# Second layer's experts: gate and bias on an expert's finished sum, second product as three rounded products, first products three blocks ahead

## The chip, the cores and the metric

One core of a Trainium2 chip runs the whole program. The time is that of one execution on the device, in microseconds (us). The engines named are TensorE (PE; its weight loads are shown apart as PEld), VectorE (DVE), ScalarE (ACT), GpSimd (POOL) and SyncE (SP), which issues the transfers.

## The reference

Four samples of 1024 tokens with 128 features go through two layers, each an attention and a mixture of experts, with a layer norm behind each of the four. The change touches the second layer's experts alone:

```
rh = gelu(x @ rW1 + rb1); p = softmax(rh @ rW2 + rb2)        # router, exact gelu
expert_weights, expert_indices = top_k(p, 2)                  # 2 of E = 4 experts
combine_w = (one_hot * expert_weights[..., None]).sum(axis=2)
for e in range(E):
    xi = x * token_mask[..., e:e + 1]
    h = gelu(xi @ We1[e] + be1[e])                            # 128 -> 512, exact gelu
    yo = h @ We2[e] + be2[e]                                  # 512 -> 128
    out = out + yo * combine_w[..., e:e + 1]                  # 0 for experts not chosen
x = layernorm(x + out)
```

All inputs and the result are float32.

## The kernel before

**Tiles and stages.** The kernel runs: first attention, the first layer's end (its output projection, norm, experts), second attention, the second layer's end. An end works on 8 chunks of 512 tokens, features on the partitions. Its experts are computed densely: 4 experts of 512 hidden features are 16 blocks of 128, n = 0 to 15, four to an expert. A block is three things: `pe_hidden` (L951) on TensorE, three rounded (float32r) matmuls that add up upper and lower halves of weights and inputs (w_hi x_hi, w_lo x_hi, w_hi x_lo) into one of four PSUM banks `hbank`; the Gelu `act_s` with bias be1 on ScalarE (L1134); and `hid`, act_s times the gate row of the expert, on VectorE (L1317). The second product (L1060) then adds w x hid in plain float32 to bank 0, over all 16 blocks, behind a bias matmul (L1058, be2 times the gates). ScalarE copies the finished sum to `y_sb` (L1141).

**Gate rows.** The router's gates of a token stand on its partition. `pe_gate_rows` (L964) spreads the gates of expert e, turned to rows in `gate_t`, over all partitions with a matmul against `expert_row` into bank 1 (L969), and ScalarE copies it to `gate_bc` (L1124). It is done at step 4e - 2, for expert 0 at step 15 of the chunk ahead.

**Order of the work.** Each engine runs its instructions in the order in which the code issues them, with semaphores between engines. `pe_chunk` (L1040), `act_chunk` (L1126) and `dve_chunk` (L1299) go through steps n = 0 to 15. At a step TensorE does its side work (`pe_beside`), a gate row, the first product of block n + h_lead (2), and the second product of block n. Side work of two other chunks is spread over the steps by `plan[1]`: for the chunk behind (back) y_turn (L979, transposes of y_sb to tokens; VectorE then adds the residual and takes statistics, L1235, L1162, L1165) and norm2 (L1170, into x_out, which SP stores); for the chunk ahead (front) os_ (L1270, a copy of the attention's output, one step before o_turn), o_turn (L890), o_proj (L1008, then on VectorE two additions and statistics, L1275, L1278), norm (L1170 into xs), x_turn (L890; ScalarE writes xt and x_hi, L1101, L1102, VectorE x_lo, L1286), hidden (L1018, the router's first product, with two Gelus rh, L1106), router (L1031, 16 small matmuls; VectorE subtracts the maximum), the exponentials e_sm on ScalarE one step later (L1113, an own table), weigh and spread on VectorE (L1207 to L1224), g_turn (L1037, then gate_t, L1116). GpSimd works out rstd from the statistics (L1348, L1349).

The stage begins in `pe_end` and its likes with the front half of chunk 0, during which ScalarE makes the upper half of the first weight, `w_hi` (L1150), and VectorE the lower, `w_lo` (L1332); SP has issued the loads of the weights we1 and we2 at L1419 and L1420. It ends with the back half of chunk 7.

Of the kernel before, what the change touches and what calls it, by code (L numbers as in the profile page):

```python
# [7 lines left out]
ALU = mybir.AluOpType  # L8
# [6 lines left out]
P = 128  # L15
# [25 lines left out]
SB = 3  # L41
PAIR_HEADS = (2, 0, 3, 1)
# [161 lines left out]
def build_program(nc, d, out):  # L204
    with ExitStack() as ctx:
# [35 lines left out]
        be2 = sb("be2", [2 * E0, D])  # L241
# [38 lines left out]
        with ExitStack() as overlay:  # L280
# [9 lines left out]
            act_s = [osb(f"act_s{i}", [P, CH]) for i in range(2)]  # L290
            lin_u = [osb(f"lin_u{i}", [P, CH]) for i in range(2)]
# [16 lines left out]
            with ExitStack() as layer_only:  # L308

                rh = layer_only.enter_context(nc.sbuf_tensor("rh", [P, 2, CH], F32))  # L310
                we2 = layer_only.enter_context(nc.sbuf_tensor("we2", [P, NH, P], F32))
# [11 lines left out]
        we2_loaded = sem("we2_loaded")  # L323
# [14 lines left out]
        class Stage:  # L338


            def __init__(self, n):
# [590 lines left out]
        for pl, steps in ((plan[0], (1, 3, 4, 5, 6, 7, 8, 9, 10, 11, None, 12, 13, 14)),  # L932
                          (plan[1], (1, 2, None, None, None, None, 2, 4, 6, 8, 10, 11, 12, 14))):
# [6 lines left out]
        h_banks, h_lead = [2, 4], [1, 2]  # L940
# [10 lines left out]
        def pe_hidden(pe, st, c, par, n, layer):  # L951

            pe.wait_ge(st.s_done, c * SPC + n + 1)
# [4 lines left out]
            for k in range(2 if layer == 0 else 1):  # L958
                for a, (w, x) in enumerate(((w_hi[k], x_hi[par]), (w_lo[k], x_hi[par]), (w_hi[k], x_lo[par]))):
                    last = nc.tensor.matmul(hbank[2 * k + n % h_banks[layer]], w[:, slice_of(n)], x[:, :], start=(a == 0),  # L960
# [11 lines left out]
        def pe_beside(pe, st, n, back, front, par, layer):  # L972

            pl = plan[layer]
            if back is not None:
                if n == pl.y_turn:
                    pe.wait_ge(st.y_saved, back + 2)
                    for t in range(TPC):
# [20 lines left out]
            if front is not None:  # L999
                if n == pl.o_turn:  # L1000
                    pe.wait_ge(st.o_in, front + 1)
                    pe_turn_tiles(bank[3], os_).then_inc(st.o_turned, 1)
# [36 lines left out]
                if n == SPC - 1:  # L1039
                    pe_gate_rows(pe, st, front, 0, layer)  # L1040

        def pe_chunk(pe, st, c, par, back, front, layer):
            per = SPC // n_exp[layer]
            w = w3 if layer == 0 else we2
            for n in range(SPC):
                pe_beside(pe, st, n, back, front, 1 - par, layer)
                e = n // per + 1
                if n % per == per - 2 and e < n_exp[layer]:
                    pe_gate_rows(pe, st, c, e, layer)
# [5 lines left out]
                if n == 0:  # L1055
                    pe.wait_ge(st.y_saved, c + 1)
                    if layer == 1:
                        nc.tensor.matmul(bank[0][:, :], be2[:, :], gate_t[:, :].bitcast(F32), start=True, stop=False)  # L1058
                pe.wait_ge(st.hid_ready, c * SPC + n + 1)
                nc.tensor.matmul(bank[0][:, :], w[:, n, :], hid[n % 2][:, :], start=(layer == 0 and n == 0),  # L1060
                                 stop=(n == SPC - 1)).then_inc(st.y_done, 1)

        def pe_end(pe, st, layer):
# [18 lines left out]
        def act_beside(act, st, n, back, front, par, layer):  # L1082
# [12 lines left out]
            if front is not None:  # L1095
# [203 lines left out]

        def dve_chunk(dve, st, c, par, back, front, layer):  # L1300
            per = SPC // n_exp[layer]
            for n in range(SPC):
                e = n // per
                if n % per == 0:
                    dve.wait_ge(st.gbc_saved, 1 + c * n_exp[layer] + e + 1)
                wait_used(dve, st.y_done, c * SPC + n - 1)
                if layer == 0:
                    dve.wait_ge(st.h_ready, c * SPC + n + 1)
# [6 lines left out]
                else:  # L1315
                    dve.wait_ge(st.s_done, h_banks[layer] + c * SPC + n + 1)
                    nc.vector.tensor_tensor(hid[n % 2][:, :], act_s[n % 2][:, :], gate_bc[e % 2][:, :],  # L1317
                                            ALU.mult).then_inc(st.hid_ready, 1)
                dve_beside(dve, st, n, back, front, 1 - par, layer)

        def dve_end(dve, st, layer):
# [18 lines left out]
            dve_chunk(dve, st, 2 * B - 1, 1, 2 * B - 2, None, layer)  # L1340
            for n in range(SPC):
# [32 lines left out]
        def _(sp):  # L1374
# [45 lines left out]
            sp.dma_start(we2[:, :, :], d["we2"]).then_inc(we2_loaded, 16)  # L1420
# [103 lines left out]
def _layout(i):  # L1524
# [38 lines left out]
    o["be2"] = np.zeros((2 * E0, D), f)  # L1563
    o["be2"][0:E1] = o["be2"][E0:E0 + E1] = a["L1_ffn_be2"]
# [14 lines left out]
```

## Time and profile before

| what | us |
|---|---|
| median of 3 runs | 1924.15 (1923.0 to 1927.66) |
| profiled execution | 1922.64 |
| its span | 1920.8 |
| TensorE busy | 1743.9 |
| VectorE busy | 1389.2 |
| ScalarE busy | 1162.8 |
| stage of the change, from os_ of chunk 0 | 1568.2 to the end |

The time of an execution is its span and 1.8 us around it. A busy share is an average over stages: what an edit is worth is read in its own stage, from what each engine waits for there. Matmuls are pipelined; the distance from one start to the next says more than the length of one. An f32 matmul of the program is shown as two instructions, a rounded one as one. The row of L513 is another stage's and stands for its kind of operation.

### The profile page before, as it was taken

The page shows a single profiled execution, that of the slowest core. Times are in us where ns is not written, and L with a number is a line of the kernel's source. Part 1 is how long each engine was busy: PE and PEld are TensorE (multiplying, and loading weights), DVE is VectorE, ACT ScalarE, POOL GpSimd, SP SyncE. Part 2 cuts the span into 40 slices and gives each one's busy share as a digit, 9 for nine tenths or more (in the row PEclk, how much of TensorE's full clock was granted, in tenths as well). Part 3 has the DMA queues.
Part 4 walks back from the last instruction along what each step waited for, and adds up shares of the span by engine and source line. Part 5 has one row for each costly group of instructions (what it writes and reads, how often), then busy time and mean ns, then how long its engine had stood idle before and what let it go on. Part 6 is the DMA issues. An engine that isn't in the chain of part 4 may idle for free.

```text
span 1920.8 us, 31169 instructions
## 1 busy us (share of the span) xinstructions
PE 1743.9 (91%) x9328; PEld 844.8 (44%) x9328; DVE 1389.2 (72%) x2540; ACT 1162.8 (61%) x1801; POOL 97.0 (5%) x123
## 2 busy tenths in 40 slices
PE   6899999699999999579999999999999968988997
PEld 3334343366656656333333333333333325544553
DVE  3788888757777777478889888989898814455544
ACT  3888888544344444107777777777777754444443
POOL 1000000001111011010000000000000000011000
PEclk9899999889999999859999999999999988999999
DMA  7532121101111000210000000000100010000000
GB/s 220 140 92 60 49 62 47 66 1 34 33 33 33 29 10 28 66 41 22 22 23 21 22 21 21 22 22 21 37 26 21 2 44 1 6 6 11 5 5 11
DMA packets 44844, 68.99 MB, mean 36 GB/s; under 512 B 15952, under 2 KB 25056, under 8 KB 44144
## 3 DMA queue, kind: packets, MB, share of 16 engines
q1 hardware_dynamic: 44784, 68.28, 11.9%
q8 instruction: 26, 0.43, 0.1%
q14 instruction: 34, 0.28, 0.1%
HBM read 42.04 MB, written 26.21 MB: 36 GB/s over the span
## 4 chain that ended last, share of the span: by engine, by line
PE 70%; DVE 12%; ACT 9%; issue 5%; SPq 1%; DMA 1%; POOL 1%; DVEq 1%; ACTq 0%; POOLq 0%
PE full_o L689 13%; PE score L676 12%; PE hid_pair L960 11%; PE bank L1060 9%; ACT probs L738 6%; PE causal_o L451 5%; PE triple L435 4%; PE max_pair L652 3%; DVE cprobs L514 2%; PE bank L969 2%; PE bank L990 2%; DVE hid L1317 1%; PE bank L890 1%; PE max_pair L663 1%; DVE negmax L776 1%
## 5 line engine op out<-in xcount | busy, mean ns | idle before, releaser
L776 DVE TENSOR_REDUCE negmax<-max_pair 128x1 f32<-128x1024 f32 x512 | 599.9, 1218 | 69.4 <-PE max_pair L652 62.3
L738 ACT ACTIVATE probs<-score 128x512 f32<-128x512 f32 x1024 | 529.0, 603 | 150.8 <-PE score L676 150.8
L652 PE MATMUL max_pair<-k_st,q_st 64*128 64x512 f32 x1024 | 405.3, 474 | 22.2 <-DMA q_st<-q_scr 18.1
L676 PE MATMUL score<-q_st,k_st 64*128 64x512 f32 x1024 | 382.9, 451 | 34.0 <-ACT probs L738 24.6
L676 PEld LDWEIGHTS score<-q_st,k_st 64*128 64x128 f32 x1024 | 170.6, 185 | 304.7 <-ACT probs L738 284.9
L484 ACT ACTIVATE cprobs<-triple 128x1536 f32<-128x1536 f32 x192 | 268.5, 1456 | 38.5 <-PE triple L435 38.3
L689 PE MATMUL full_o<-probs,v_st 128*32 128x512 f32 x2048 | 272.9, 606 | 0.0
L960 PE MATMUL hid_pair<-x_hi,w_hi 128*128 128x512 f32 x384 | 206.8, 539 | 0.0
L652 PEld LDWEIGHTS max_pair<-k_st,q_st 64*128 64x128 f32 x1024 | 171.7, 191 | 79.5 <-DVE negmax L776 39.5
L1132 ACT ACTIVATE act_s<-hid_pair 128x512 f32<-128x512 f32 x128 | 76.4, 597 | 157.5 <-PE hid_pair L960 157.4
L514 DVE TENSOR_SCALAR cprobs<-cprobs 128x1536 f32<-128x1536 f32 (+6 forms) x272 | 163.0, 624 | 0.4 <-ACT cprobs L484 0.4
L451 PE MATMUL causal_o<-cprobs,v_st 128*32 128x512 f32 (+3 forms) x1536 | 154.5, 498 | 8.4 <-DVE o_sb L539 7.0
L1060 PE MATMUL bank<-hid,we 128*128 128x512 f32 x256 | 137.0, 618 | 20.4 <-DVE hid L1317 20.4
L960 PE MATMUL hid_pair<-x_lo,w_hi 128*128 128x512 f32 x384 | 154.0, 401 | 0.0
L960 PE MATMUL hid_pair<-x_hi,w_lo 128*128 128x512 f32 x384 | 153.6, 400 | 0.0
L435 PE MATMUL triple<-q_st,k_st 64*128 64x512 f32 (+3 forms) x768 | 143.8, 400 | 8.3 <-ACT cprobs L484 5.0
L1317 DVE TENSOR_TENSOR hid<-act_s,gate_bc 128x512 f32<-128x512 f32 x128 | 85.1, 688 | 90.8 <-ACT act_s L1134 79.2
L1309 DVE TENSOR_TENSOR lin_u<-hid_pair,gate_bc 128x512 f32<-128x512 f32 x128 | 88.3, 690 | 74.9 <-PE hid_pair L960 68.9
L1060 PE MATMUL bank<-hid,w 128*128 128x512 f32 x256 | 132.2, 598 | 0.9 <-DVE hid L1313 0.7
L435 PEld LDWEIGHTS triple<-q_st,k_st 64*128 64x128 f32 x768 | 73.5, 187 | 116.0 <-issue 64.8
L513 DVE SCALAR_TENSOR_TENSOR cprobs<-cprobs,bound 128x512 f32<-128x512 f32 (+4 forms) x176 | 94.9, 539 | 16.0 <-ACT cprobs L484 10.5
L1124 ACT ACTIVATE gate_bc<-bank 128x512 f32<-128x512 f32 x96 | 57.4, 598 | 79.7 <-PE bank L969 79.5
(129 smaller groups left out, 1594.0 us busy)
## 6 DMA issues: line engine op xcount, KB each, us to landing
k_st<-k_scr SPq DMA_DIRECT2D x64, 128.0 KB, 2.8
q_st<-q_scr SPq DMA_DIRECT2D x128, 64.0 KB, 2.3
q_st<-q_scr SPq DMA_DIRECT2D x16, 512.0 KB
k_st<-k_scr SPq DMA_DIRECT2D x64, 104.0 KB
q_scr<-qk_hi SPq DMA_DIRECT2D x24, 256.0 KB, 2.9
k_scr<-qk_hi SPq DMA_DIRECT2D x24, 256.0 KB, 3.1
q_scr<-qk_lo SPq DMA_DIRECT2D x16, 256.0 KB, 2.9
k_scr<-qk_lo SPq DMA_DIRECT2D x16, 256.0 KB, 3.2
```

Of the source, the lines that this page charges most:

```text
L435: last = nc.tensor.matmul(triple[n % 2][:, bk, off:off + w], k_st[p][rows, j, kt * P:(kt + 1) * P], q_st[p][rows, q0:q0 + w], start=True, ...
L451: last = nc.tensor.matmul(causal_o[SLOT * j:SLOT * (j + 1), c0:c0 + w], v_st[p][:, kt, j, :], cprobs[at % CP][:, bk, off:off + w], start=( ...
L484: nc.scalar.activation(cprobs[n % CP][:, :, :], triple[n % 2][:, :, :], ACT.Exp, scale=SCALE).then_inc(L.exp_done, 1)
L514: ins = nc.vector.tensor_scalar(plain, plain, float(np.exp(-CLIP)), float(np.exp(CLIP)), ALU.max, ALU.min)
L652: ins = nc.tensor.matmul(ring[slot][:, half, :], q_st[p][rows, qt * P:(qt + 1) * P], k_st[p][rows, j, half * CH:(half + 1) * CH], start=Tr ...
L676: nc.tensor.matmul(sbank[L.score_bank(e)][:, :], k_st[p][rows, j, kt * P:(kt + 1) * P], q_st[p][rows, q0:q0 + w], start=True, stop=True, t ...
L689: last = nc.tensor.matmul(full_o[SLOT * j:SLOT * (j + 1), :], v_st[p][:, kt, j, :], probs[s % NP][:, j, :], start=(kt == 0), stop=last_ste ...
L738: nc.scalar.activation(probs[s % NP][:, j, :], sbank[L.score_bank(e)][:, :], ACT.Exp, scale=SCALE).then_inc(L.exp_done, 1)
L776: nc.vector.tensor_reduce(negmax[:, qt // TPC, j, qt % TPC:qt % TPC + 1], ring[slot][:, :, :].rearrange("p a n -> p (a n)"), AXX, ALU.max, ...
L960: last = nc.tensor.matmul(hbank[2 * k + n % h_banks[layer]], w[:, slice_of(n)], x[:, :], start=(a == 0), stop=(a == 2))
L1060: nc.tensor.matmul(bank[0][:, :], w[:, n, :], hid[n % 2][:, :], start=(layer == 0 and n == 0), stop=(n == SPC - 1)).then_inc(st.y_done, 1)
L1317: nc.vector.tensor_tensor(hid[n % 2][:, :], act_s[n % 2][:, :], gate_bc[e % 2][:, :], ALU.mult).then_inc(st.hid_ready, 1)
```

## The change

The second weight we2 is now split into upper and lower halves like we1, and so is hid: on even blocks ScalarE writes the rounded upper half `hid_hi` itself with a second Gelu from the same bank, on odd blocks VectorE copies it from act_s; VectorE then writes `hid_lo` = act_s - hid_hi. There are four buffers of each. The gate is not applied to hid any more: an expert's four blocks are summed alone, into bank 0 for even experts and hbank[3] for odd ones, and `dve_weigh` adds the bias be2 (a column now, transposed on the host side of the layout) and multiplies by the gate row; experts 1 to 3 go through `y_tmp` and an addition into y_sb. The weighing of expert e stands at step 4e + 5, that of expert 3 at step 1 of the next chunk. First products run three blocks ahead in three banks (`h_of`, `h_apart`: where two blocks that use one bank are two apart, the wait is for the Gelu two before). Gate row e is made at step 4e + 2. y_turn moves from step 1 to 3, norm2 from 2 to 5, g_turn from 14 to 15. The bias matmul and ScalarE's copy of y_sb go in this layer.

```diff
-                          (plan[1], (1, 2, None, None, None, None, 2, 4, 6, 8, 10, 11, 12, 14))):
+                          (plan[1], (3, 5, None, None, None, None, 2, 4, 6, 8, 10, 11, 12, 15))):
...
-        h_banks, h_lead = [2, 4], [1, 2]
+        h_banks, h_lead = [2, 3], [1, 3]
+
+        y_bank = [bank[0][:, :], hbank[3]]
+        h_of = [[n % 2 for n in range(SPC)], [n % 3 if n < SPC - 1 else 1 for n in range(SPC)]]
+        h_apart = [[2] * SPC, [2 if n in (1, SPC - 1) else 3 for n in range(SPC)]]
...
-            pe.wait_ge(st.s_done, c * SPC + n + 1)
+            pe.wait_ge(st.s_done, c * SPC + n + 1 + h_banks[layer] - h_apart[layer][n])
...
                     pe.wait_ge(st.y_saved, back + 2)
+                    if layer == 1 and front is not None:
+                        pe.wait_ge(st.ot_ready, front + 1)
...
                     pe.wait_ge(st.o_in, front + 1)
+                    if layer == 1 and back is not None:
+                        pe.wait_ge(st.gate_t, front)
...
+        def pe_gate_step(pe, st, c, n, layer):
+            per = SPC // n_exp[layer]
+            e = n // per + (layer == 0)
+            if n % per == per - 2 and e < n_exp[layer]:
+                pe_gate_rows(pe, st, c, e, layer)
...
+        def pe_split_product(pe, st, c, n):
+            per = SPC // E1
+            e, f = n // per, n % per
+            if f == 0:
+                wait_used(pe, st.y_used, c * E1 + e - 1)
+            pe.wait_ge(st.hid_ready, c * SPC + n + 1)
+            hi, lo = hid_hi[n % HB], hid_lo[n % HB]
+            for a, (w, x) in enumerate(((w_hi[1], hi), (w_lo[1], hi), (w_hi[1], lo))):
+                last = nc.tensor.matmul(y_bank[e % 2], w[:, slice_of(n)], x[:, :], start=(f == 0 and a == 0),
+                                        stop=(f == per - 1 and a == 2))
+            last.then_inc(st.y_done, 1)
...
-                    if layer == 1:
-                        nc.tensor.matmul(bank[0][:, :], be2[:, :], gate_t[:, :].bitcast(F32), start=True, stop=False)
...
             act.wait_ge(st.gbc_ready, c * n_exp[layer] + e + 1)
-            wait_used(act, st.hid_ready, c * SPC + (e - 1) * (SPC // n_exp[layer]))
+            if layer == 0:
+                wait_used(act, st.hid_ready, c * SPC + (e - 1) * (SPC // E0))
+            else:
+                wait_used(act, st.y_used, c * E1 + e - 1)
...
-                    nc.scalar.activation(act_s[n % 2][:, :], hbank[n % h_banks[1]], ACT.Gelu,
+                    if n % 2 == 0:
+                        wait_used(act, st.y_done, c * SPC + n - HB + 1)
+                        nc.scalar.activation(hid_hi[n % HB][:, :], hbank[h_of[1][n]], ACT.Gelu, bias=be1[:, n:n + 1])
+                    nc.scalar.activation(act_s[n % 2][:, :], hbank[h_of[1][n]], ACT.Gelu,
                                          bias=be1[:, n:n + 1]).then_inc(st.s_done, 1)
...
-                    for k in range(2 if layer == 0 else 1):
-                        act.wait_ge(raw_loaded[k], 16 * (layer + 1) if k == 0 else 16)
+                    for k in range(2):
+                        act.wait_ge(raw_loaded[k], 16 * (layer + 1))
...
+        def dve_weigh(dve, st, c, e):
+            dve.wait_ge(st.gbc_saved, 1 + c * E1 + e + 1)
+            dve.wait_ge(st.y_done, c * SPC + (e + 1) * (SPC // E1))
+            if e == 0:
+                wait_used(dve, st.y_turned, c)
+            elif e > 1:
+                dve.wait_ge(st.y_sum, 2 * c + e - 1)
+            nc.vector.scalar_tensor_tensor((y_sb if e == 0 else y_tmp)[:, :], y_bank[e % 2], be2[:, e:e + 1],
+                                           gate_bc[e % 2][:, :], ALU.add, ALU.mult).then_inc(st.y_used, 1)
+            if e > 0:
+                dve.wait_ge(st.y_used, c * E1 + e + 1)
+                nc.vector.tensor_tensor(y_sb[:, :], y_sb[:, :], y_tmp[:, :],
+                                        ALU.add).then_inc(st.y_sum if e < E1 - 1 else st.y_saved, 1)
...
+                    wait_used(dve, st.y_done, c * SPC + n - HB + 1)
                     dve.wait_ge(st.s_done, h_banks[layer] + c * SPC + n + 1)
-                    nc.vector.tensor_tensor(hid[n % 2][:, :], act_s[n % 2][:, :], gate_bc[e % 2][:, :],
-                                            ALU.mult).then_inc(st.hid_ready, 1)
+                    if n % 2 == 1:
+                        nc.vector.tensor_copy(hid_hi[n % HB][:, :], act_s[n % 2][:, :]).then_inc(st.odd_hi, 1)
+                        dve.wait_ge(st.odd_hi, c * (SPC // 2) + n // 2 + 1)
+                    nc.vector.tensor_tensor(hid_lo[n % HB][:, :], act_s[n % 2][:, :], hid_hi[n % HB][:, :].bitcast(F32),
+                                            ALU.subtract).then_inc(st.hid_ready, 1)
+                    if n % per == 1 and (n > per or back is not None):
+                        dve_weigh(dve, st, c if n > per else back, (e - 1) % E1)
...
-                    for k in range(2 if layer == 0 else 1):
+                    for k in range(2):
                         dve.wait_ge(w_upper, 2 * layer + k + 1)
...
-            sp.dma_start(we2[:, :, :], d["we2"]).then_inc(we2_loaded, 16)
+            sp.dma_start(w_raw[1][:, :], d["we2"].rearrange("p n c -> p (n c)")).then_inc(raw_loaded[1], 16)
```

## Rows read from the trace of the kernel before

**Rows 1.** The page, busy time of each engine and the granted clock.

```profile
PE 1743.9 (91%) x9328; PEld 844.8 (44%) x9328; DVE 1389.2 (72%) x2540; ACT 1162.8 (61%) x1801; POOL 97.0 (5%) x123
...
PEclk9899999889999999859999999999999988999999
```

**Rows 2.** Windows cut at the router's product: busy, (instructions), clock, DMA share, GB/s.

```profile
1625.20:1666.56 41.36, 37.93 (x134) 21.09 (x132) 21.25 (x70) 18.89 (x31) 3.65 (x4) 0.96 0.02 7
1666.56:1706.90 40.34, 36.27 (x133) 20.23 (x132) 21.37 (x70) 18.77 (x31) 3.63 (x4) 1.00 0.03 8
```

**Rows 3.** Waits, 1621 to 1866 us: total us, times, longest.

```profile
PEld bank L1060 <- DVE hid L1317: 32.0, 30, 2.2
...
PEld bank L890 <- DVE os_ L1270: 10.8, 6, 1.8
```

**Rows 4.** Groups of instructions by form, 1621 to 1866 us; the last one of the whole span.

```profile
L1317 DVE TENSOR_TENSOR hid<-act_s,gate_bc 128x512 f32<-128x512 f32 x96 | 63.8, 687 | 61.0 <-ACT act_s L1134 56.1 <-PE bank L1060 4.0
L1134 ACT ACTIVATE act_s<-hid_pair,be 128x512 f32<-128x512 f32 x96 | 62.3, 689 | 19.3 <-PE hid_pair L960 12.6 <-DVE hid L1317 6.6
...
L1058 PE MATMUL bank<-gate_t,be 16*128 16x512 f32 x12 | 6.7, 640 | 0.0
...
L513 DVE SCALAR_TENSOR_TENSOR cprobs<-cprobs,bound 128x512 f32<-128x512 f32 x48 | 32.8, 684 | 0.0
```

**Rows 5.** Timeline: two blocks in a row (start us, length us, engine).

```profile
1605.25 1.02 PE L1060 MATMUL bank<-hid,we 128*128 128x512 f32 x2
...
1606.35 0.40 PE L960 MATMUL hid_pair<-x_hi,w_lo 128*128 128x512 f32 x1
...
1606.58 0.40 PE L960 MATMUL hid_pair<-x_lo,w_hi 128*128 128x512 f32 x1
...
1606.82 1.02 PE L1060 MATMUL bank<-hid,we 128*128 128x512 f32 x2
```

**Rows 6.** Timeline: TensorE's side work: o_proj, a gate row and what follows, the router's two products.

```profile
1607.68 1.05 PE L1008 MATMUL bank<-w_o,ot 128*128 128x128 f32 x8
...
1613.41 0.49 PE L969 MATMUL bank<-gate_t,expert_row 16*128 16x512 f32 x1
...
1614.17 0.39 PE L960 MATMUL hid_pair<-x_hi,w_lo 128*128 128x512 f32 x1
...
1621.15 1.88 PE L1018 MATMUL bank<-xt,rw 128*128 128x512 f32 x4
...
1625.04 1.84 PE L1031 MATMUL bank<-rw,rh 128*128 128x4 f32 x16
```

**Rows 7.** Timeline: ScalarE at the exponentials, beside the router.

```profile
1626.00 1.28 ACT L1113 ACT_TABLE_LOAD   x1
...
1627.54 0.22 ACT L1113 ACTIVATE e_sm<-sc 128x16 f32<-128x16 f32 x1 [0.26 <-DVE sc L1186]
...
1629.07 1.27 ACT L1134 ACTIVATE act_s<-hid_pair,be 128x512 f32<-128x512 f32 x2
```

**Rows 8.** Timeline: VectorE's side work in steps 1, 4 and 6.

```profile
1640.17 0.69 DVE L1235 TENSOR_TENSOR res<-xs,bank 128x512 f32<-128x512 f32 x1 [1.05 <-PE bank L979]
...
1642.21 0.39 DVE L1270 COPY os_<-o_tm 128x512 f32 x1
...
1648.62 0.69 DVE L1275 TENSOR_TENSOR res<-x_tm,bank 128x512 f32<-128x512 f32 x1 [1.70 <-PE bank L1008]
...
1651.38 1.28 DVE L1317 TENSOR_TENSOR hid<-act_s,gate_bc 128x512 f32<-128x512 f32 x2
...
1653.60 1.11 DVE L1170 TENSOR_SCALAR xs<-res,mv,rstd 128x128 f32<-128x128 f32 x4 [0.93 <-POOL rstd L1349]
```

**Rows 9.** The second weight's load (KB, us to landing), w_lo at the start, and y_sb at the end.

```profile
we<-in_we SPq DMA_DIRECT2D x1, 1024.0 KB, 7.4
...
1578.28 2.28 DVE L1332 TENSOR_TENSOR w_lo<-w_raw,w_hi 128x2048 fp32r<-128x2048 f32 x1
...
1911.17 0.60 ACT L1141 ACTIVATE y_sb<-bank 128x512 f32<-128x512 f32 x1 [2.08 <-PE bank L1060]
```

More of the change, by code:

```diff
@@ L290, in build_program @@
             act_s = [osb(f"act_s{i}", [P, CH]) for i in range(2)]
+            with ExitStack() as layer_only:
+                hid_hi = [layer_only.enter_context(nc.sbuf_tensor(f"hid_hi{i}", [P, CH], F32R)) for i in range(HB)]
             lin_u = [osb(f"lin_u{i}", [P, CH]) for i in range(2)]
@@ L310, in build_program @@
                 rh = layer_only.enter_context(nc.sbuf_tensor("rh", [P, 2, CH], F32))
-                we2 = layer_only.enter_context(nc.sbuf_tensor("we2", [P, NH, P], F32))
+                hid_lo = [layer_only.enter_context(nc.sbuf_tensor(f"hid_lo{i}", [P, CH], F32R)) for i in range(HB)]
+                y_tmp = layer_only.enter_context(nc.sbuf_tensor("y_tmp", [P, CH], F32))
         q_scr0 = nc.dram_tensor("q_scr0", [B, P, 2, T], F32, kind="Internal").ap()
@@ L959, in pe_hidden @@
                 for a, (w, x) in enumerate(((w_hi[k], x_hi[par]), (w_lo[k], x_hi[par]), (w_hi[k], x_lo[par]))):
-                    last = nc.tensor.matmul(hbank[2 * k + n % h_banks[layer]], w[:, slice_of(n)], x[:, :], start=(a == 0),
+                    last = nc.tensor.matmul(hbank[2 * k + h_of[layer][n]], w[:, slice_of(n)], x[:, :], start=(a == 0),
                                             stop=(a == 2))
@@ L1054, in pe_chunk @@
                     pe_hidden(pe, st, front, 1 - par, lead - SPC, layer)
-                if n == 0:
-                    pe.wait_ge(st.y_saved, c + 1)
-                    if layer == 1:
-                        nc.tensor.matmul(bank[0][:, :], be2[:, :], gate_t[:, :].bitcast(F32), start=True, stop=False)
-                pe.wait_ge(st.hid_ready, c * SPC + n + 1)
-                nc.tensor.matmul(bank[0][:, :], w[:, n, :], hid[n % 2][:, :], start=(layer == 0 and n == 0),
-                                 stop=(n == SPC - 1)).then_inc(st.y_done, 1)
+                if layer == 0:
+                    if n == 0:
+                        pe.wait_ge(st.y_saved, c + 1)
+                    pe_product(pe, st, c, n)
+                else:
+                    pe_split_product(pe, st, c, n)
         def pe_end(pe, st, layer):
@@ L1066, in pe_end @@
                 pe_beside(pe, st, n, None, 0, 0, layer)
-            pe.wait_ge(w_lower, 2 if layer == 0 else 3)
-            if layer == 1:
-                pe.wait_ge(we2_loaded, 16)
+            pe.wait_ge(w_lower, 2 * (layer + 1))
             for n in range(h_lead[layer]):
@@ L1116, in act_beside @@
                     nc.scalar.activation(gate_t[:, :], bank[3][0:2 * E0, :], ACT.Copy).then_inc(st.gate_t, 1)
-                if n == SPC - 1:
+                if n == SPC - 1 and layer == 0:
                     act_gate_rows(act, st, front, 0, layer)
@@ L1303, in dve_chunk @@
                 e = n // per
[L1304 to L1306 removed]
                 if layer == 0:
+                    if n % per == 0:
+                        dve.wait_ge(st.gbc_saved, 1 + c * n_exp[layer] + e + 1)
+                    wait_used(dve, st.y_done, c * SPC + n - 1)
                     dve.wait_ge(st.h_ready, c * SPC + n + 1)
@@ L1340, in dve_end @@
             dve_chunk(dve, st, 2 * B - 1, 1, 2 * B - 2, None, layer)
+            if layer == 1:
+                dve_weigh(dve, st, 2 * B - 1, E1 - 1)
             for n in range(SPC):
```

31 lines of the change are left out of this document (18 added, 13 removed).

## The prediction

> **What bounds the kernel now.** I read the page first [rows 1]: TensorE is busy for 91% of the span, VectorE for 72%, ScalarE for 61%. These shares mix four stages; the edits touch the second layer's expert stage alone, the last 325 us. So I cut that stage at the first router product (L1031) of each chunk [rows 2]. The first cut to the last is 1625.20 to 1870.22, six chunks, 40.84 us each. Two lengths alternate: 41.5 us where the granted clock is 0.96 and 40.2 us where it is 1.00, so one stretch at the lower level (1.2 of 2.4 GHz) costs some 1.3 us. VectorE works 21.3 us of such a chunk, ScalarE 18.8; TensorE is the busy one.
>
> The waits of these six chunks [rows 3] say what TensorE's idle time is: the second product L1060 waits for hid 30 times, 32.0 us, and the first transposes of the o tiles for VectorE's copy, 10.8 us. The timeline [rows 5] gives the bare block: L1060 starts at 1605.25, the next at 1606.82, so 1.57 us. A rounded matmul takes 0.23 us (1606.35 to 1606.58), a triple 0.69, so L1060 in f32 takes 1.57 - 0.69 = 0.88 us. Sixteen blocks are 25.1 us; the work beside them, read in the same way [rows 6], is 0.9 for the o projection, 1.7 for the router's first product, 1.8 for its second, 0.6 for each of four gate rows (from 1613.35, where the product before ends, to 1613.94, where the next triple starts: its second matmul stands at 1614.17), and 0.45 for each of four groups of four transposes, half of the o projection's eight matmuls: 8.6 us. With the bias matmul (0.9) that is 34.6; the other 5.6 of a 40.2 us chunk are waits.
>
> **What the change takes from TensorE.** The second product becomes three rounded matmuls, 0.69 for 0.88: 16 x 0.19 = 3.0 us a chunk. The bias matmul L1058 (two instructions a chunk, [rows 4]) goes: 0.9. TensorE's own work falls from 34.6 to 30.7 us. If nothing else bound, eight chunks would give 31 us.
>
> **What it puts on VectorE.** The hid product becomes the subtraction hid_lo: same shape, 0.69 long, 0.61 from start to start (two in 1.29). Added for each of 8 odd blocks is a rounding copy and a wait for it. The trace has no 128x512 rounding copy on VectorE. Its bounds are the f32 copy from SBUF, 0.39 to 0.42 [rows 8], and the one-element-a-cycle operation, 0.69; I take 0.42 plus 0.04, as the operands lie in SBUF. The Trainium skill ("VectorE: DVE Perf Modes", What auto-detection actually checks) makes the faster mode a matter of one source, both sides in SBUF, not of the type's name; by it the copy is 0.42, by the slow bound each chunk has 8 x 0.27 = 2.2 us more on VectorE. Four weighings a chunk are a scalar_tensor_tensor (0.68, [rows 4]) and an addition 0.61 to 0.69, with the wait 1.35 together: 5.4 us. So VectorE goes from 21.3 to about 21.3 + 3.7 + 5.4 = 30.4 us, as much as TensorE's 30.7. ScalarE gets 8 Gelus more (0.58 each) and loses one copy: 18.8 to 23. Two engines of 30.5 us that feed each other through buffers of 3 or 4 blocks don't run in 30.5; what counts is where they meet.
>
> **The walk through a chunk.** Time 0 is the end of the router's second product: 1.8 after 1625.04, so 1626.83 in the trace. Every latency is from the timeline: ScalarE starts 0.2 after a triple ends, 0.05 after a semaphore; gate_bc to the next act_s 0.48; a TensorE instruction that really waited loses 0.15 more, its weights not being loaded ahead.
>
> Steps 12 to 15. ScalarE has two Gelus for block 12 now and is done at 0 instead of -0.8. Loading Exp's table takes 1.28, e_sm 0.22, the Gelu table 1.28 [rows 7]: act_s 13 starts at 2.7 (before: 2.24) and ends at 3.4. Hidden block 15 shares its bank with block 13, so TensorE, free at 1.4, waits for that until 3.5. Product 12 ends at 5.0, 13 at 6.4, gate row 3 at 7.0. act_s 15 stands behind the gate_bc copy on ScalarE: 8.15; hidden 1 of the next chunk needs it and ends at 9.05, product 14 at 9.75. g_turn, 15 now, has its gates since 7.4; ends at 10.2, product 15 at 11.6. On ScalarE the two Gelus of block 0 stand behind the gate_t copy (10.25): done at 12.0; hidden 3 waits 0.6 for that. Product 1 ends at 15.0 (before it began at 13.84, so ended at 14.7). This far nothing is won.
>
> Steps 1 to 3. VectorE's hid_lo 1 is done at 13.7, weighing 3 at 15.1, the os_ copy behind it at 15.46; o_turn waits 0.5 (before: 1.1, behind the statistics). Gate_bc, act_s 3, copy and subtraction give hid 3 at 19.05, product 3 ends at 20.0.
>
> Steps 3 to 7 are VectorE's. From 19.0 it has no gap: y_turn's addition and statistics 2.04 (1640.17 to 1642.21), hid 4, the o projection's part 2.76 (1648.62 to 1651.38), hid 5 with its copy 1.08, weighing 0 1.35, norm2 1.05, hid 6, norm 1.05 (a 1.11 row, [rows 8]), hid 7 with its copy. So hid 4 is ready at 21.7, 5 at 25.5, 6 at 28.5, 7 at 30.6, and TensorE waits 0.3, 2.4, 1.0 and 0.7 us; product 7 ends at 31.5. The longer lead can't hide it: block n's Gelu is possible only once product n-3 is about to start, some 3 us ahead, and this stretch has 11.6 us on VectorE against 7.0 on TensorE (0.9 + 0.6 + four blocks of 1.38).
>
> Steps 8 to 10. x_turn ends at 31.95; xt and x_hi on ScalarE, then act_s 9 at 33.8, for which hidden 12 waits 0.6; hid 9 at 35.0; product 9 ends at 35.9, the router's first product at 37.6, and gate row 0.6, two triples' worth 1.38 and the second product 1.78 make 41.4. Against 40.84 that is **+0.56 a chunk**, six times: +3.4 us. (Against the chunks at full clock, 40.2, it is +1.2: 3.9 us won in work, 5.1 lost in waits.)
>
> **The ends of the stage.** Start: the first gate row falls out of the way to hidden 0, and product 0 ends about 1.5 us earlier; of this the step 5 and 9 waits of chunk 0, walked alike without y_turn and norm2, leave 0.6 at its router's end: -0.6. The second weight's DMA is the size of we2's and landed in 7.4 us, at 1575.8 [rows 9]; its w_hi copy of 1.9 us ends before x_turn's xt at 1579.57, and the second w_lo, 2.28 like the first, ends near 1583, under the router's products, long before hidden 0 at 1596.4: 0; uncovered it would be 2 us. Last chunk: no front half; walked alike product 15 ends 39.1 after its zero; before it was 39.3 (from 1871.85 to 1911.15, where y_sb follows, [rows 9]): -0.2. Then y_sb is not one copy (0.60 at 1911.17) but the last weighing, 1.35: +0.7.
>
> **The clock.** Low stretches come after TensorE's waits: the ones before follow product 5's wait. TensorE will wait about 10.7 us a chunk instead of 5.6, so I count one low stretch in every chunk; it falls partly where VectorE decides, so 0.5 of 1.3 us: +3.5 (bounds 0 and +9).
>
> **Sum.** 3.4 - 0.6 - 0.2 + 0.7 + 3.5 = +6.8 on the profiled execution's 1922.64 (span 1920.8 and 1.8 around it): 1929.4. It lies 1.5 below the median of 1924.15, so 1931 for the median, 0.35% slower. Differences under 0.3% (5.8 us) can't be told from none.
>
> **Rivals.** (A) The waits don't build up and TensorE's saving shows. It would be so if TensorE carried a lead into step 3: the waits of steps 4 to 7 (4.4 us) and for block 15 (2.1) halve, a chunk takes 38.2: seven times -2.6, 1905 to 1910. For it: half of the sum of before's waits is of the kinds that go (o tiles, y_sb before L1058). Against: ScalarE and VectorE work in a fixed order, and act_s 3 stands behind a gate_bc of step 2 whatever the lead. Chance 0.2. (B) It cancels: the Exp step costs less, as act_s 13 gets in sooner, a chunk takes 40.6 and the clock's term is near 0: 1921 to 1928. Chance 0.3. (C) the forecast, a chunk of 41 to 42 us: 1929 to 1937, chance 0.38. (D) As C but the rounding copy at 0.69: six of its eight (blocks 1, 3, 5, 7, 9, 13) are on the path, 6 x 0.27 = 1.6 a chunk, +11: 1942; chance 0.12. A ends on the other side; it decides from the point where hid 5 is ready less than 22.4 after the router.
>
> The likeliest is C, with its own range 1929 to 1937; 1905 to 1944 leaves out a part of A and of D. Slower 0.5, same 0.3, faster 0.2.
>
> **What would show it.** After the change: chunks, router to router, of 41 to 42 us; VectorE busy 30 us of each and without gaps from y_turn's addition to norm; second products 4 to 7 waiting for hid_lo, 4 to 5 us together; hidden block 15 waiting 2 us for act_s behind the Exp table. The copy's row reads 0.42 or 0.69 at once. Chunks under 40 us make it wrong, and so would a second product's triple that isn't 0.69 us.

## The result, and the profile after

The changed kernel takes 1942.36 us (median of 4 runs, 1937.9 to 1947.94) against 1923.58 us: a ratio of 1.0114, 95% interval 1.0093 to 1.0134, so slower by 1.1%. The forecast was 1931, slower by 0.35%. A second timing (e12 below) gave 1.0116.

The page of the changed kernel, as [rows 1] of before:

```profile
PE 1743.1 (90%) x9440; PEld 882.1 (45%) x9440; DVE 1454.3 (75%) x2661; ACT 1196.4 (61%) x1858; POOL 95.7 (5%) x123
...
PEclk8899999899999999759999999999999969889988
```

TensorE is as busy as before though it got less work. The profiled execution is the slowest of the four, 1947.94 us, 25.3 above the one of before. The same cut as [rows 2], at the first matmul of the router's second product (L1045 now, L1031 before). The first row is chunk 0 and the last row the last chunk with the tail (columns: us, then busy time and instructions of PE, PEld, DVE, ACT, POOL, granted clock, DMA share, GB/s):

```profile
1590.54:1629.72 39.18, 31.76 (x119) 23.23 (x119) 19.44 (x60) 18.19 (x30) 1.65 (x2) 0.79 0.00 1
1629.72:1672.99 43.27, 35.83 (x146) 24.91 (x145) 29.15 (x85) 22.80 (x38) 3.29 (x4) 0.92 0.02 7
1672.99:1717.57 44.58, 37.66 (x146) 25.89 (x144) 29.11 (x85) 22.83 (x38) 3.22 (x4) 0.89 0.02 6
1717.57:1762.55 44.98, 37.45 (x146) 25.85 (x145) 29.35 (x85) 22.95 (x38) 3.29 (x4) 0.89 0.02 7
1762.55:1804.08 41.53, 34.56 (x146) 23.86 (x145) 29.03 (x85) 22.82 (x38) 3.22 (x4) 0.96 0.02 7
1804.08:1847.43 43.35, 35.81 (x145) 24.61 (x144) 29.34 (x85) 22.93 (x38) 3.29 (x4) 0.92 0.02 7
1847.43:1891.96 44.53, 37.64 (x145) 25.82 (x144) 29.22 (x85) 22.80 (x38) 3.23 (x4) 0.89 0.02 6
1891.96:1946.10 54.14, 37.90 (x151) 25.79 (x149) 35.27 (x94) 25.01 (x40) 3.52 (x4) 0.87 0.03 10
```

The same two rows of the kernel before, chunk 0 and the last chunk with the tail:

```profile
1585.91:1625.04 39.13, 32.32 (x108) 19.59 (x109) 15.32 (x52) 15.59 (x25) 1.79 (x2) 0.83 0.00 1
...
1870.06:1920.80 50.74, 39.61 (x134) 21.57 (x132) 23.38 (x72) 19.86 (x31) 2.77 (x4) 0.96 0.04 11
```

The six whole chunks take 43.71 us on average (1629.72 to 1891.96) instead of 40.84: 6 x 2.87 = 17.2 us. The last chunk and tail take 54.1 instead of 50.7, 3.4. The stretch of chunk 0 is equal, 39.2 and 39.1. The other 4.6 us lie ahead of the stage of the change: its first instruction, the os_ copy of chunk 0, starts at 1572.87, before at 1568.24, and from there to the first row it is 17.67 us in both. The edits are to the second layer's experts, not to what runs ahead of them, and in the profiled executions of the experiments below it starts anywhere from 1563.7 (e8) to 1572.1 (e11), at 1570.3 in e12, the same kernel again. So these 4.6 us vary from one execution to another; what makes them vary isn't shown.

The column of the granted clock is what to read here. The chunks of 41.5, 43.3 and 44.5 to 45.0 us have a clock of 0.96, 0.92 and 0.89. A chunk at clock k has spent (1 - k) / 0.5 of its time at the lower level: 3.3, 6.9 and 9.8 us. Where these low stretches lie is seen in windows of 2 us. One in the first whole chunk, then one in the second:

```profile
1658.00:1660.00 2.00, 2.00 (x6) 1.09 (x5) 2.00 (x7) 0.63 (x2) 0.54 (x1) 0.61 0.00 0
...
1664.00:1666.00 2.00, 2.00 (x9) 1.61 (x9) 0.00 (x0) 0.45 (x1) 0.00 (x0) 0.68 0.00 0
...
1680.00:1682.00 2.00, 2.00 (x6) 1.59 (x5) 1.86 (x6) 0.00 (x0) 0.00 (x0) 0.50 0.00 0
```

Read through the whole stage, they lie at two places. One is behind product 5's wait, some 28 to 30 us into the chunk, in every chunk: 3.4 us long in the chunk from 1762.55 and 6.8 us in the five others (before, every second chunk had one of 3.4 there). The other is behind hidden 15's wait, some 5.5 us into the chunk: 3.4 us, in the second, third and sixth whole chunk and in the last. So the three kinds of chunk are product 5 short, product 5 long, and product 5 long with hidden 15. Why a stretch is long, and why the same wait of hidden 15 is followed by none in three chunks, isn't shown.

### The profile page after: what moved, and what is told of

It is laid out like the page before. It is cut to its first block and busy times, and to the rows that moved or that the text cites. A ratio compares the mean times of both kernels' runs of the same rounds, so it can differ in the third digit from the quotient of the medians.

```text
span 1946.1 us, 31707 instructions
## 1 busy us (share of the span) xinstructions
PE 1743.1 (90%) x9440; PEld 882.1 (45%) x9440; DVE 1454.3 (75%) x2661; ACT 1196.4 (61%) x1858; POOL 95.7 (5%) x123
## 5 line engine op out<-in xcount | busy, mean ns | idle before, releaser
L970 PE MATMUL hid_pair<-x_hi,w_hi 128*128 128x512 f32 x384 | 187.8, 489 | 28.2 <-ACT act_s L1173 28.2
L970 PEld LDWEIGHTS hid_pair<-x_hi,w_hi 128*128 128x128 f32 x384 | 75.5, 197 | 78.1 <-ACT act_s L1173 39.9
L1376 DVE TENSOR_TENSOR hid_lo<-act_s,hid_hi 128x512 fp32r<-128x512 f32 x128 | 88.0, 689 | 26.4 <-ACT act_s L1173 24.1
```

The lines of the kernel that those rows point to most:

```text
L970: last = nc.tensor.matmul(hbank[2 * k + h_of[layer][n]], w[:, slice_of(n)], x[:, :], start=(a == 0), stop=(a == 2))
```

## The walk against the trace

The chunk from 1762.55 is the one with the least time at the low level. TensorE's waits in it (timeline; the last bracket is the idle time before and its releaser), to be read from the router's end, 1762.55 + 1.78 = 1764.33:

```profile
1767.81 0.50 PE L970 MATMUL hid_pair<-x_hi,w_hi 128*128 128x512 f32 x1 [1.95 <-ACT act_s L1173]
...
1772.56 0.50 PE L970 MATMUL hid_pair<-x_hi,w_hi 128*128 128x512 f32 x1 [1.27 <-ACT act_s L1173]
...
1786.45 0.47 PE L1078 MATMUL hid_pair<-hid_hi,w_hi 128*128 128x512 f32 x1 [0.15 <-DVE hid_lo L1376]
...
1790.16 0.50 PE L1078 MATMUL hid_pair<-hid_hi,w_hi 128*128 128x512 f32 x1 [2.08 <-DVE hid_lo L1376]
...
1798.29 0.51 PE L970 MATMUL hid_pair<-x_hi,w_hi 128*128 128x512 f32 x1 [0.36 <-ACT act_s L1173]
...
1799.55 0.50 PE L1078 MATMUL bank<-hid_hi,w_hi 128*128 128x512 f32 x1 [0.30 <-DVE hid_lo L1376]
```

Hidden 15 starts at +3.48, hidden 1 at +8.23, product 4 at +22.1, product 5 at +25.8, hidden 12 at +34.0, product 9 at +35.2. The walk, with its 0.15 after a real wait, had 3.6, 8.35, 21.9, 25.7, 33.95 and 35.2. VectorE in steps 3 to 7, in the first whole chunk:

```profile
1650.69 0.68 DVE L1275 TENSOR_TENSOR res<-xs,bank 128x512 f32<-128x512 f32 x1
...
1653.08 0.69 DVE L1376 TENSOR_TENSOR hid_lo<-act_s,hid_hi 128x512 fp32r<-128x512 f32 x1
1653.69 0.68 DVE L1315 TENSOR_TENSOR res<-x_tm,bank 128x512 f32<-128x512 f32 x1
...
1656.45 0.41 DVE L1374 CAST hid_hi<-act_s 128x512 fp32r<-128x512 f32 x1
1656.89 0.69 DVE L1376 TENSOR_TENSOR hid_lo<-act_s,hid_hi 128x512 fp32r<-128x512 f32 x1
1657.50 0.74 DVE L1348 SCALAR_TENSOR_TENSOR y_sb<-bank,be,gate_bc 128x512 f32<-128x512 f32 x1
1658.16 1.11 DVE L1210 TENSOR_SCALAR x_out<-res,mv,rstd 128x128 f32<-128x128 f32 x4
1659.19 0.68 DVE L1376 TENSOR_TENSOR hid_lo<-act_s,hid_hi 128x512 fp32r<-128x512 f32 x1
1659.79 1.11 DVE L1210 TENSOR_SCALAR xs<-res,mv,rstd 128x128 f32<-128x128 f32 x4
1660.82 0.42 DVE L1374 CAST hid_hi<-act_s 128x512 fp32r<-128x512 f32 x1
```

From y_turn's addition to the copy of block 7, 10.1 us, VectorE is never idle for more than 0.21 us. The rounding copy is a CAST of 0.41 to 0.43 (the bound of 0.69 is out), the subtraction 0.69, and the weighing's first instruction 0.74, not the 0.68 of [rows 4], where all operands lie in SBUF.

## The experiments

Each ratio is against the kernel before on the same chip, with its 95% interval. "A chunk" is the mean of six, router to router, in the profiled execution.

**e1: unread matmuls in TensorE's waits.** The edit, with the wait on the last gate copy that keeps bank 1 free:

```diff
+        FILL = {5: 8, 6: 3, 7: 2, 12: 7}
+            pe.wait_ge(st.gbc_saved, c * E1 + (n - 3) // 4 + 2)
+            for _ in range(FILL[n]):
+                nc.tensor.matmul(bank[1][:, :], w_hi[0][:, slice_of(0)], x_hi[par][:, :], start=True, stop=True)
```

> The changed kernel with rounded 128x512 matmuls that nobody reads, put into bank 1 where TensorE waits: 8 before product 5's wait, 3 at the start of step 6, 2 before product 7's wait, 7 at the start of step 12 (0.23 us each at full clock, inside waits of 2 us that the changed kernel's trace shows). Theory K (what the forecast mis-sized is the clock: the low stretches behind these waits cost some 2 us a chunk): the granted clock in the stage rises from 0.90 to 0.96 or more, a chunk falls from 43.7 to about 42, the ratio to the kernel before from 1.0114 to 1.003 to 1.006. Rival W (the waits themselves are longer than the walk had them, the clock only follows): chunks stay at 43.5 or grow by what of the fillers sticks out, ratio 1.011 to 1.016.

1930.32 us, ratio 1.0059 (1.0044 to 1.0075). Its six chunks, and the last one:

```profile
1623.45:1664.79 41.34, 37.37 (x165) 26.38 (x164) 29.36 (x85) 22.80 (x38) 3.29 (x4) 1.00 0.02 7
1664.79:1705.94 41.15, 37.62 (x165) 26.39 (x164) 29.23 (x85) 22.80 (x38) 3.22 (x4) 1.00 0.02 7
1705.94:1747.44 41.50, 37.32 (x165) 26.38 (x164) 29.36 (x85) 22.96 (x38) 3.29 (x4) 1.00 0.03 8
1747.44:1788.54 41.10, 37.60 (x165) 26.38 (x164) 29.23 (x85) 22.79 (x38) 3.22 (x4) 1.00 0.02 7
1788.54:1830.02 41.48, 37.35 (x165) 26.38 (x164) 29.36 (x85) 22.95 (x38) 3.29 (x4) 1.00 0.02 7
1830.02:1871.11 41.09, 37.56 (x166) 26.39 (x165) 29.23 (x85) 22.80 (x38) 3.22 (x4) 1.00 0.02 7
1871.11:1927.30 56.19, 41.59 (x178) 29.60 (x176) 35.30 (x94) 25.01 (x40) 3.52 (x4) 0.92 0.03 10
```

TensorE does 20 matmuls more in each chunk, 4.6 us of them, and the chunk falls from 43.71 to 41.28, with the clock at 1.00 throughout. Nothing of the computation was taken away, and TensorE's 24 waits for the Gelu and 12 for hid_lo in the six chunks are still there, only shorter. So 2.4 us of each chunk were the clock's, and 41.3 is what the waits alone make of it: the walk had 41.4. In the last chunk the fillers stick out (56.2 against 54.1).

Chunk against the same chunk, this prices the low stretches of the changed kernel. The short one behind product 5 costs 0.4 us (41.53 against 41.10), the long one 1.9 (43.27 against 41.34, 43.35 against 41.48), and long with hidden 15's 3.4 to 3.5 (44.58, 44.98 and 44.53 against 41.15, 41.50 and 41.09). So the first 3.4 us behind product 5 cost 0.4, every further 3.4 us 1.5.

**e2: norm2 at step 10.** One number in the plan, 5 to 10.

> The changed kernel with one number changed: norm2 (1.05 us on VectorE, four tensor_scalars) from step 5 to step 10, where VectorE has slack. Theory D (steps 3 to 7 are VectorE's, as in the walk): blocks 6 and 7 are ready 1.05 us sooner, a chunk is 1.0 us shorter at the same clock, more if a low stretch goes too: ratio 1.0114 falls to about 1.007. Rival P (TensorE at its low clock sets the pace of these steps): no change, 1.010 to 1.012.

1938.34 us, 1.0102 (1.0088 to 1.0117): the time is the rival's (1.010 to 1.012), not the theory's 1.007, although the mean chunk fell to 42.65 (43.71 in the changed kernel, 43.18 in e12's execution of it). Two chunks of it, then two windows of 2 us in the second of them:

```profile
1668.11:1711.12 43.01, 36.07 (x146) 24.70 (x145) 29.23 (x85) 22.82 (x38) 3.16 (x4) 0.92 0.02 7
1711.12:1753.51 42.39, 34.71 (x146) 23.78 (x145) 29.36 (x85) 22.94 (x38) 3.24 (x4) 0.96 0.02 7
```

```profile
1717.00:1719.00 2.00, 2.00 (x6) 1.55 (x5) 1.93 (x4) 0.48 (x1) 0.00 (x0) 0.50 0.02 4
...
1741.00:1743.00 2.00, 2.00 (x8) 1.21 (x8) 1.99 (x6) 0.81 (x2) 0.59 (x1) 1.00 0.00 0
```

From product 5's start to the router's first product it takes 9.03 us, in the changed kernel's 1762.55 chunk 10.19: the 1.05 of norm2 are won where the walk said. But the chunk at 0.96 takes 42.4, not 41.5. Its low stretch lies at 1716 to 1720, just behind hidden 15's wait, where TensorE sets the pace: gate row 3 starts 8.0 after the router's end instead of 6.5. In the changed kernel's chunk at 0.96 it lies behind product 5's wait (1791 to 1795), where VectorE sets the pace by the walk, and costs the 0.4 of e1.

**e3: the second product in float32 again.** ScalarE writes the Gelu straight to four float32 buffers:

```diff
-            for a, (w, x) in enumerate(((w_hi[1], hi), (w_lo[1], hi), (w_hi[1], lo))):
+            nc.tensor.matmul(y_bank[e % 2], w_raw[1][:, slice_of(n)], hid_lo[n % HB][:, :], start=(f == 0),
...
-                    nc.vector.tensor_tensor(hid_lo[n % HB][:, :], act_s[n % 2][:, :], hid_hi[n % HB][:, :].bitcast(F32),
-                                            ALU.subtract).then_inc(st.hid_ready, 1)
```

> The changed kernel with its rounding undone: the second product is one float32 matmul of we2 with ScalarE's Gelu (four buffers, written straight by ScalarE), so VectorE has neither hid nor halves to make, ScalarE 16 Gelus instead of 24. Gate and bias on an expert's sum, the lead of three blocks and the plan stay. TensorE's own work is 33.7 us a chunk, VectorE's 21.3 - 9.8 + 5.4 = 17. Theory D (VectorE and ScalarE in series with TensorE set the chunk): the waits of steps 4 to 7 go, a chunk takes 36 to 38 us, and the kernel 1893 to 1907, ratio 0.984 to 0.991, better than both. Rival T (TensorE's work counts first): 3 us more work a chunk than the changed kernel, so slower than it, above 1.012.

1893.57 us, 0.987 (0.9856 to 0.9885), faster than both kernels. A chunk, and TensorE's two long waits in it:

```profile
1657.09:1693.92 36.83, 34.10 (x129) 20.28 (x128) 15.91 (x61) 17.95 (x30) 2.53 (x4) 1.00 0.03 8
```

```profile
1661.86 0.50 PE L970 MATMUL hid_pair<-x_hi,w_hi 128*128 128x512 f32 x1 [1.27 <-ACT hid_lo L1170]
...
1666.92 0.50 PE L970 MATMUL hid_pair<-x_hi,w_hi 128*128 128x512 f32 x1 [1.26 <-ACT hid_lo L1170]
```

The three rounded products save TensorE 3 us a chunk; leaving them out saves 43.71 - 36.84 = 6.9, of which 2.4 are the clock's (e1) and 4.4 are left with both at 1.00. VectorE has 16.0 us of work instead of 29.2, and the waits for hid are gone. What is left are the waits of hidden 15 and hidden 1 for ScalarE.

**e4: the lead of three alone,** in the kernel before (`h_lead` [1, 2] to [1, 3]).

> The kernel before with one part of the change alone: first products three blocks ahead (four banks as before). hid has two buffers, so VectorE can't run further ahead. Theory D: the waits of before come from bursts on VectorE and from order on ScalarE, which a longer lead leaves: 0 to -0.5 us a chunk, ratio 0.998 to 1.000. Rival L (the lead itself hides waits): -2 us a chunk, ratio 0.993.

1919.57 us, 1.0015 (1.0001 to 1.0029): no gain (0.998 to 1.000 expected). Chunks:

```profile
1663.56:1703.90 40.34, 36.29 (x131) 20.23 (x130) 21.37 (x70) 18.66 (x31) 3.63 (x4) 1.00 0.03 8
1703.90:1745.16 41.26, 37.80 (x132) 21.10 (x130) 21.31 (x70) 18.72 (x31) 3.35 (x4) 0.96 0.02 6
```

The same 40.3 and 41.3 as in [rows 2]. (Its mean is 40.51 since one low stretch of three is missing in that execution: its fifth chunk takes 39.90 at 1.00, against 41.53 at 0.96 before.)

**e5: e3 with other banks.** Two blocks that share a bank are two apart at 4 and 6 instead of at 15 and 1:

```diff
+        turn = [n % 3 if n < SPC - 1 else 1 for n in range(SPC)]
+        h_of = [[n % 2 for n in range(SPC)], [turn[(n + 11) % SPC] for n in range(SPC)]]
+        h_apart = [[2] * SPC, [2 if n in (4, 6) else 3 for n in range(SPC)]]
```

> The f32 kernel of the last study (e3, ratio 0.987) with the place changed where two blocks that use one PSUM bank are two apart: blocks 4 and 6 instead of 15 and 1. In e3's trace hidden 15 and hidden 1 wait 1.3 us each for a Gelu that stands behind the Exp table and behind the gate_bc copy. Theory S (TensorE waits there for ScalarE's order, and nothing is late behind it): both waits go, a chunk falls from 36.84 to 34.3 to 34.8 us, ratio 0.978 to 0.980. Rival R (the same Gelus are needed for the products a step later, so the wait only moves): less than 0.5 us a chunk, ratio 0.985 to 0.987.

1871.33 us, 0.9747 (0.9731 to 0.9763), a chunk 33.97, both better than expected (0.978, 34.3):

```profile
1652.42:1686.39 33.97, 33.77 (x129) 20.29 (x128) 15.88 (x61) 17.98 (x30) 2.53 (x4) 1.00 0.03 9
```

TensorE is busy for 33.77 of 33.97 us: its own work, 33.7 by the sum, sets the chunk. The wait did not move, it went.

**e6: the fillers in the kernel before,** six ahead of product 5.

> The kernel before with six unread rounded matmuls in bank 1 ahead of product 5's wait for hid (1.46 us in the trace). Theory K (the wait of product 5 lets the clock fall in every second chunk): all six chunks take 40.2 at a granted clock of 1.00, mean 40.84 falls to 40.2, ratio 0.997 to 0.999. Rival W: the chunks still alternate, or lose what sticks out of the wait.

1919.08 us, 0.9994 (0.9982 to 1.0006). The verdict alone can't tell; the chunks can:

```profile
1625.52:1665.23 39.71, 37.64 (x138) 21.35 (x137) 21.23 (x70) 18.75 (x31) 3.65 (x4) 1.00 0.03 8
1665.23:1705.56 40.33, 37.66 (x138) 21.34 (x137) 21.35 (x70) 18.76 (x31) 3.63 (x4) 1.00 0.02 7
```

The clock no longer alternates; the mean is 40.00 at a clock of 1.00, so the low stretches inside 40.84 were 0.84 us a chunk (expected 0.64). Chunk against the same chunk, the three that had a low stretch fall from 41.36, 41.56 and 41.53 to 39.71, 39.92 and 39.90, and the three others stay within 0.04. So a stretch of 3.4 us costs 1.64 in the kernel before, at the same wait of product 5 where it costs 0.4 in the changed one. Behind that wait TensorE has no other for 9 us in the kernel before (product 5 at 1652.12, the next wait at 1661.54, 0.26 us). The prediction's 1.3 came from comparing odd with even chunks, which differ by 0.2 to 0.6 without it. The last chunk lost 1.3 us to fillers that stuck out (52.1 against 50.7), which takes back a part of it.

**e7: the changed kernel with e5's banks,** nothing else.

> The changed kernel with the same change of banks as e5 and nothing else. Theory D (walk): hidden 15 and hidden 1 no longer wait (2.1 + 1.35 us), but product 14 then waits for hid_lo 14 at 8.1 and product 0 for ScalarE's gate_t as before: 0.5 to 1.5 us a chunk are won: ratio 1.003 to 1.009. Rival S (TensorE's waits for ScalarE are additive to the rest): 3 us a chunk, ratio 1.000 or less.

1927.59 us, 1.0037 (1.0023 to 1.0051). All six chunks are like this one:

```profile
1664.40:1705.42 41.02, 35.04 (x146) 23.63 (x145) 29.03 (x85) 22.79 (x38) 3.21 (x4) 0.96 0.02 7
```

A rotated table wins two thirds of the loss. The ratio is in the theory's range, but the chunk won 2.6 us where 0.5 to 1.5 were expected: 41.07 at a clock of 0.96 compares with 41.5 in the changed kernel's chunk at 0.96, so the waits themselves give 0.4 us and the low time that went (one short stretch a chunk is left, behind product 5) the other 2.2. The last chunk and tail fall too, from 54.1 to 51.7.

**e8: every upper half by ScalarE.** `if n % 2 == 0` goes on ScalarE, the copy and its wait on VectorE.

> The changed kernel with every hid_hi written by ScalarE with a second Gelu: VectorE loses 8 rounding copies of 0.42 and their waits (3.7 us a chunk), ScalarE gets 8 Gelus of 0.58 (4.6 us). Theory D (VectorE's stretch in steps 3 to 7 sets the pace): three copies go from the stretch, 1.4 us, and ScalarE's longer chain costs 0.3 at three other places: a chunk 0.5 to 1.5 us shorter, ratio 1.004 to 1.009. Rival S (ScalarE's order is the chain): a chunk 1 to 2 us longer, ratio 1.016 or more.

1950.31 us, 1.0153 (1.0139 to 1.0168). My expectation failed, the rival's holds: a chunk takes 44.7, 1.0 more than in the changed kernel. One of them:

```profile
1754.71:1799.03 44.32, 36.26 (x145) 24.57 (x144) 26.03 (x77) 27.16 (x46) 3.13 (x4) 0.92 0.02 6
```

How long TensorE's weight loads waited for the Gelu (total us, times, longest), e8 first (1631 to 1890 us, which leaves out the first of its 24 waits), then the changed kernel (1631 to 1893 us):

```profile
PEld hid_pair L970 <- ACT act_s L1173: 42.8, 23, 3.5
```

```profile
PEld hid_pair L970 <- ACT act_s L1173: 33.8, 24, 2.4
```

VectorE has 3.2 us less work in each chunk, and TensorE waits longer for ScalarE.

**e9: e7 with fillers in steps 5 to 7,** none in the last chunk.

> The changed kernel with e7's banks and e1's unread matmuls in steps 5, 6 and 7 (not in step 12, where e7 has no long wait left, and not in the last chunk). Theory K (the clock and the waits are separate terms): e7's chunks of 41.07 us at a clock of 0.96 lose their one low stretch, 0.5 to 1.3 us: 39.8 to 40.6, ratio 0.999 to 1.002. Rival: the stretch lies where VectorE decides and costs nothing, 41.0 and 1.0037.

1921.72 us, 1.0005 (0.9995 to 1.0016), a chunk 40.71, a little above the 39.8 to 40.6 expected:

```profile
1663.44:1704.05 40.61, 36.43 (x159) 25.02 (x158) 29.20 (x85) 22.79 (x38) 3.21 (x4) 1.00 0.02 7
```

The one low stretch per chunk that e7 had left cost 0.36 us, as the short one behind product 5's wait did in e1. So the waits of the changed kernel with better banks are worth about as much as its rounded products save: no change.

**e10: rounded products on even blocks only,** on top of e5: `if n % 2 == 1` takes e3's float32 product, otherwise the three rounded ones.

> e5 (gate on the sum, f32 second product, banks of 4 and 6) with the three rounded products kept for the even blocks alone: ScalarE writes hid_hi and act_s there, VectorE only subtracts; odd blocks stay f32. TensorE's work falls by 8 x 0.19 = 1.5 us, VectorE gets 8 x 0.61 = 4.9, ScalarE 8 x 0.58 = 4.6. Theory T (with slack on both other engines TensorE's saving shows): a chunk of 32.5 to 33 us, ratio 0.967 to 0.971. Theory D (each added step in the chain Gelu, halves, product gives back what it saves): 33.5 to 36 us, ratio 0.973 to 0.985.

1896.87 us, 0.988 (0.9865 to 0.9896); a chunk 37.47, slower than e5 by 3.5 and worse than either theory had it (33.5 to 36 for the slower one).

```profile
1692.99:1730.61 37.62, 34.08 (x138) 21.43 (x137) 20.71 (x69) 22.70 (x38) 2.79 (x4) 1.00 0.02 7
```

TensorE has 1.5 us less to do than in e5 (by the sum 32.2), VectorE 20.7 us and ScalarE 22.7 of a chunk of 37.5, and yet TensorE waits. The granted clock is 1.00, so it isn't the clock either. That the order does it, not the amount, is the reading that is left; no run takes the order apart from the added steps.

**e11: e5 with the lead of two.**

> e5 with the first products two blocks ahead instead of three. Theory D (the lead mattered only because VectorE stood between Gelu and product): 34.0 to 34.5 us a chunk, ratio 0.975 to 0.978. Rival L (the lead is what hides ScalarE's order): 35 to 37 us, ratio above 0.981.

1872.39 us, 0.9747 (0.9731 to 0.9764), a chunk 33.50 (34.0 to 34.5 expected):

```profile
1689.66:1723.17 33.51, 33.51 (x129) 20.47 (x128) 15.96 (x61) 18.26 (x30) 2.54 (x4) 1.00 0.03 8
```

The ratio is e5's, and the chunk is no longer than e5's 33.97. The lead of three is worth nothing here, where VectorE does not stand between Gelu and product, as it was worth nothing in e4.

**e12: the changed kernel again.**

> The changed kernel once more, unchanged, on this chip. All theories: ratio 1.010 to 1.013, as the first time (1.0114); its profile shows whether a chunk still takes 43 to 44 us and how the low stretches vary from one execution to another: with theory K the mean chunk moves with the mean granted clock, along 0.5 us of time for each us spent low.

1941.28 us, 1.0116 (1.0097 to 1.0135), a chunk 43.18. Two chunks in a row:

```profile
1710.39:1755.35 44.96, 37.36 (x146) 25.84 (x144) 29.35 (x85) 22.97 (x38) 3.29 (x4) 0.89 0.02 7
1755.35:1796.79 41.44, 34.51 (x146) 23.83 (x145) 29.03 (x85) 22.80 (x38) 3.22 (x4) 0.96 0.02 7
```

Its chunks at 0.96 take 41.4 and 41.8, at 0.92 43.0 and 43.4, at 0.88 and 0.89 44.5 and 45.0. Against the same chunks of e1 they are 0.3 to 0.4, 1.9 and 3.4 to 3.5 longer, as in the first execution. So my "0.5 us for each us spent low" holds nearly (1.5 for 3.4) for all but the first 3.4 us behind product 5.

## Why the prediction was wrong

- **The direction and its reason were right.** TensorE's saving is given back in waits for VectorE and ScalarE; e3 shows it from the other side. The walk's 41.4 us a chunk is 41.3 in e1, where the clock stays high, and its single steps came within 0.25 us.
- **The mis-sized term is the clock's.** It was put at +3.5 us with +9 as the bound, one low stretch in every chunk of which 0.5 of 1.3 counts. Measured: 43.71 - 41.28 = 2.4 us a chunk, 14.6 us over six, in the profiled execution; 43.18 and 11.4 in e12's. The count was wrong: a chunk spends 3.3 to 9.8 us at the low level, not one stretch of 3.3, since the one behind product 5's wait lasts 6.8 us in five chunks of six, and hidden 15's wait, which the walk itself had, brings another in three. (Hidden 1's wait, which it had too, brings none.) And the price was wrong: 0.5 is right for a single stretch behind product 5's wait (0.4), but each further 3.4 us, there or behind hidden 15's wait, costs 1.5 (e1, e2). The 1.3 from which it was taken is itself 1.64 (e6). A fall of the clock did not need long waits here: no matmul of the six chunks waited longer than 2.1 us. The Trainium skill ("TensorE: Matmul & The Clock Gate", A second HAM failure mode: psum-queue depth-cycling) tells of a kernel whose short idles between groups of matmuls were frequent enough to make the clock swing; this trace agrees. I had weighed no more than the one kind of stretch in [rows 2].
- **The ends of the stage.** -0.6 for the start did not come in this execution (39.18 against 39.13), where chunk 0 has a low stretch more, at 1617 to 1621, and a clock of 0.79 instead of 0.83. In e12's, with a clock of 0.82, it is there (38.52). Splitting the second weight cost nothing, as forecast: 17.67 us from os_ to the router's second product in both kernels. The last chunk and tail were +0.5 and are +3.4. In the tail the last weighing is 0.75 and 0.69 in place of a copy of 0.60. The last chunk and tail spend some 14 us at the low level instead of 4 (0.87 and 0.96); how much of the 3.4 that makes isn't shown, as e1's fillers stuck out there. With e7's banks it is 51.7, at 0.94.
- **The sum.** Forecast 3.4 - 0.6 + 0.5 + 3.5 = 6.8. Measured in the profile 2.6 (6 x 0.44) for the waits, 14.6 for the clock, 0.05 for the start, 3.4 for the end: 20.7, and 4.6 ahead of the stage. The medians differ by 18.8. In this sum, as in the forecast's, the 40.84 of before holds its own low stretches. With both kernels at a clock of 1.00 (e1, e6) the chunk goes from 40.00 to 41.28, so of the 2.87 us lost per chunk 1.3 are waits and 1.6 are the clock.
- **Rivals.** A and B did not come. D's time came (1942) by luck, without its cause: the copy is 0.42 long. The rule of the Trainium skill ("VectorE: DVE Perf Modes", What auto-detection actually checks) that the prediction went by, one source and both sides in SBUF, agrees with this rounding copy too (0.42 us).
- **What was not seen.** How cheap two of the largest waits were to remove: a rotated table of banks (e7), and that the weighing of a finished sum, with the old product, was the better change (e3, e5).

## What to carry to other kernels

A wait of TensorE can have two prices, its length and the low clock behind it. The second was small only where another engine set the pace anyway: 3.4 us at the low level behind product 5's wait cost 0.4 in the changed kernel and 1.64 in the one before, where TensorE ran on for 9 us without a wait. So walk the order, mark who sets the pace behind each wait, and charge it at the others. Matmuls that nobody reads, put into the waits, measure it: more work, less time. Work saved on the busiest engine was lost here when it was bought with steps in the ring that feeds it (e3, e10), however idle the other engines looked. Take work out of that ring first, as the gate on four sums in place of sixteen blocks does, and put the reuse of banks where the order has slack. (e11 has both, with a few steps of the plan moved and the float32 product and the lead of two of the kernel before, and is 2.5% faster; e5 against e3 prices the banks, the gate on the sums has no run of its own.)

## What was not expected of the hardware

Low stretches of the clock followed waits of 1.5 to 2.1 us, though not each of them, and a kernel with 20 more matmuls a chunk ran 0.55% faster than without (1.0059 against 1.0114). scalar_tensor_tensor of 128x512 with PSUM and SBUF tensors took 0.745 us where the form with SBUF operands took 0.684. A float32 copy and one that rounds to float32r take the same 0.42 us on VectorE.
